# Expert slots that begin behind the last weighing, with the last utterance's routing laid between them

## The chip, the cores and the metric

The kernel runs on one core of a Trainium2 chip. The metric is the device time of one launch in microseconds (us), the median of several launches. Lower is better.

## What is computed

Sixteen utterances of 750 frames with 23 features go through one audio layer. A context-5 projection makes 746 tokens of 128 channels for each utterance, 11,936 in all, with batch normalisation behind it. Then come an attention block with 8 heads of 16 channels and a feed-forward layer with 8 experts, of which each token uses exactly one:

```python
h = _L0_tok_ref(x, W, b, gamma, beta)
h = h + _L0_attn_ref(_layernorm(h), ...)      # softmax(q k^T / 4) v, 8 heads, then Wo
# _L0_ffn_ref(_layernorm(h), ...):
router_logits = xf @ Wr + br
topk_logits, topk_idx = jax.lax.top_k(router_logits, 1)
topk_gates = jax.nn.softmax(topk_logits, axis=1)
for e in range(8):
    hh = jax.nn.relu(xf @ W1[e] + b1[e])      # 128 -> 512
    oe = hh @ W2[e] + b2[e]                   # 512 -> 128
    out = out + jnp.where((idx_k == e)[:, None], gate_k * oe, 0.0)
```

## The kernel before, in words

Every engine has a program of its own, written out by hand; semaphores (`s_...`) tie the programs together. B = 16 utterances, D = 128, NT = 6 token tiles for an utterance, STEPS = 96.

**Bodies.** `run_bodies` writes 19 bodies, i = -2 to 16. Body i runs the 96 attention steps of utterance i on TensorE (score matmuls, L1247, and weighings of the values, L1312), the exponentials on ScalarE (L808), and the score maxima of a coming utterance on VectorE (L1112). Between the steps stand, at numbered places, the projections for utterance i + 2 and the routing of utterance i - 1: output projection (task PROJ), residual, layer norm statistics, router, ranks (task RANK), and six indirect DMAs on GpSimd, which scatter the token rows to `routed_rows_dram`, sorted by expert (L631). Body 16, LAST_BODY, has no attention step of its own: it holds the last weighing's drain and the routing of utterance 15, one instruction after the other.

**Slots.** The sorted rows are worked off in 101 slots of 128 rows with one expert each (`run_slots`, L361). For a slot SyncE loads the rows (L561); TensorE transposes them (`x_t_slot`, L1382), runs `layer1` (L1391, four matmuls) and `layer2` (L1401, four matmuls); ScalarE copies the transpose out (L861) and does the relu (L852, four instructions); VectorE copies the expert's weights, 1,156 numbers a partition, for the slot three further on (L1097), adds the bias (L1209) and applies gate and residual (L1214); GpSimd scatters the result to the output (`store_slot`, L720). Rows and results have a ring of 6 buffers, weights one of 3. VectorE's turn s waits until the store of slot s - 6 has landed, and SyncE's load of slot s until VectorE has finished slot s - 6. In TensorE's turn s stand layer1 of slot s + 1, the transpose of slot s + 2 and layer2 of slot s.

**Two tables** tell which expert and which rows a slot has. The early table covers the slots that are full with what had been ranked when it was made (EARLY = 78 of them, made in body 16 out of utterances 0 to 14). The late table (L1168 to L1192) covers the rest. Slots 0 to 11 are written out; behind slot 5 VectorE makes the late table in one piece, and behind slot 11 it is put in place. Then SyncE writes eight blocks of pad rows (`pad_regions`, L424 and L425) and waits for them before it loads slot 12. Slots 12 up to the last few are a hardware loop (`Fori`) with six slots in its body, on every engine.

## Time and profile before

| | us |
|---|---|
| median of 3 runs (lowest, highest) | 1274.9 (1272.45, 1276.98) |
| profiled execution, span from first to last instruction | 1275.9 |
| TensorE busy in the span | 1178.7 (92%) |
| VectorE busy | 1072.5 (84%) |
| ScalarE busy | 950.6 (75%) |
| GpSimd busy | 680.0 (53%) |

For the profiled execution no device time is listed beside its span; the span lies 1.0 us above the median and inside the three runs. Busy shares are averages over stages with different limits. The bodies end at about 1033 us, and the slots run from 1048 us to the end; the two have to be read apart. In rows of instructions the first two numbers are start and duration, the bracket at the end is the engine's idle time before the row and what released it. PEclk is TensorE's granted clock as a share of 2.4 GHz. "remote" and "issue" mean that the profile shows no releaser on this core.

### The profile page before, as it was taken

The numbers are of one execution on the slowest core, as the hardware profiler recorded it, in microseconds if no ns is written. First come the engines' busy times: TensorE is split into PE (matmuls) and PEld (weight loads), VectorE is DVE, ScalarE is ACT, GpSimd is POOL, SyncE is SP. The second block draws the span as 40 slices with busy tenths as digits, with TensorE's granted clock in tenths as the row PEclk, the third lists the DMA queues.
The fourth block names the chain that finished last, engine by engine and source line by source line (L and its number), as shares of the span: only waits on it lengthen the run. The fifth ranks groups of instructions, "written<-read, shape, count | busy, mean of one in ns | idle before, by whom it ended". The sixth has DMA issues, their size and how long they took to land.

```text
span 1275.9 us, 53879 instructions
## 1 busy us (share of the span) xinstructions
PE 1178.7 (92%) x21379; PEld 745.5 (58%) x21379; DVE 1072.5 (84%) x2756; ACT 950.6 (75%) x2477; POOL 680.0 (53%) x894
## 2 busy tenths in 40 slices
PE   6479999999999999999999999999999846899996
PEld 3334656555555556555555556565644326899996
DVE  7469899999999999999999999999999544577774
ACT  4426988888887878788888878797877824567774
POOL 2062436566473837475665739374723334456664
PEclk9768999999999999999999999999999969899998
DMA  8152132222313131323223131313220513333331
GB/s 190 39 84 79 40 86 72 76 84 61 94 52 94 45 105 42 104 72 79 83 63 93 51 94 45 106 41 104 72 80 28 150 56 105 88 93 105 103 101 50
DMA packets 79409, 102.32 MB, mean 80 GB/s; under 512 B 15916, under 2 KB 72995, under 8 KB 78734
## 3 DMA queue, kind: packets, MB, share of 16 engines
q1 hardware_dynamic: 70624, 79.02, 23.4%
q0 software_dynamic: 8384, 20.22, 5.1%
q8 instruction: 158, 2.59, 0.9%
q14 instruction: 57, 0.47, 0.1%
q10 hardware_dynamic: 186, 0.02, 0.0%
HBM read 60.76 MB, written 38.93 MB: 78 GB/s over the span
## 4 chain that ended last, share of the span: by engine, by line
PE 63%; DVE 20%; issue 5%; POOL 3%; ACT 2%; DMA 1%; SPq 1%; another core or an unknown queue 1%; POOLq 0%; DVEq 0%; ACTq 0%
PE psum L1247 36%; DVE half_max L1112 14%; PE psum L1312 13%; PE psum L1391 6%; PE psum L1401 5%; PE psum L1252 2%; ACT arena L808 2%; DVE stats L916 1%; POOL out_dram L720 1%; DVE rows L990 1%; PE psum L1382 1%; POOL arena L405 1%; DMA arena<-max_rows 1%; PE psum L1267 1%; DVE arena L962 1%
## 5 line engine op out<-in xcount | busy, mean ns | idle before, releaser
L1112 DVE TENSOR_REDUCE half_max<-psum 128x1 f32<-128x373 f32 x1536 | 760.8, 534 | 62.8 <-PE psum L1247 55.0
L808 ACT ACTIVATE arena<-psum 128x373 f32<-128x373 f32 (+1 forms) x1536 | 655.0, 489 | 154.4 <-PE psum L1247 139.0
L1247 PE MATMUL psum<-k_rows,arena 96*32 96x373 bf16 x6144 | 519.1, 329 | 14.9 <-DVE half_max L1112 6.1
L1247 PE MATMUL psum<-arena,k_rows 98*32 98x373 bf16 x6144 | 515.7, 326 | 13.7 <-ACT arena L808 6.2
L1312 PE MATMUL psum<-arena,values 128*32 128x373 f32 (+1 forms) x3072 | 313.2, 478 | 0.2
L1247 PEld LDWEIGHTS psum<-k_rows,arena 96*32 96x32 bf16 x6144 | 173.8, 96 | 195.7 <-DVE half_max L1112 103.4
L1247 PEld LDWEIGHTS psum<-arena,k_rows 98*32 98x32 bf16 x6144 | 176.4, 95 | 178.2 <-ACT arena L808 74.8
L631 POOL DMA_INDIRECT routed_rows_dram<-rows,pos_i x96 | 96.6, 1007 | 170.7 <-PE psum L1247 106.2
L720 POOL DMA_INDIRECT out_dram<-arena,slot_id x101 | 119.2, 1180 | 90.0 <-issue 51.5
L1312 PEld LDWEIGHTS psum<-arena,values 128*32 128x32 f32 (+1 forms) x3072 | 98.4, 110 | 20.7 <-issue 2.8
L861 ACT COPY arena<-psum 128x128 f32<-128x128 f32 x101 | 26.9, 266 | 77.7 <-PE psum L1382 39.7
L639 POOL TENSOR_TENSOR m_diff<-stats 128x6 f32<-128x6 f32 x15 | 3.1, 203 | 147.1 <-DVE stats L916 147.1
L1391 PE MATMUL psum<-arena,seq 128*128 128x128 f32 x544 | 75.3, 283 | 5.1 <-issue 2.4
L852 ACT ACTIVATE arena<-psum,seq 128x128 f32<-128x128 f32 x272 | 77.8, 370 | 0.5 <-issue 0.5
L1401 PE MATMUL psum<-seq,arena 128*128 128x128 f32 x544 | 73.8, 280 | 0.3 <-ACT arena L852 0.3
L1391 PEld LDWEIGHTS psum<-arena,seq 128*128 128x128 f32 x544 | 69.1, 199 | 6.5 <-issue 5.0
L405 POOL TENSOR_SCALAR arena<-h_cur,m_mean,rstd 128x128 f32<-128x128 f32 x90 | 70.9, 800 | 3.3 <-POOL rstd L665 3.3
L405 POOL TENSOR_SCALAR rows<-rows,n_mean,rstd 128x128 f32<-128x128 f32 x90 | 70.8, 796 | 0.0
L1401 PEld LDWEIGHTS psum<-seq,arena 128*128 128x128 f32 x544 | 67.6, 195 | 0.5 <-ACT arena L852 0.5
L1097 DVE COPY seq<-seq 128x1156 f32 x68 | 53.6, 788 | 11.1 <-issue 1.4
L950 DVE STREAM_TRANSPOSE by_tok<-o_un 128x384 f32<-128x384 f32 x64 | 36.2, 566 | 18.7 <-ACT o_un L817 18.7
L1209 DVE TENSOR_TENSOR arena<-psum,seq 128x128 f32<-128x128 f32 x68 | 19.8, 291 | 35.3 <-PE psum L1401 30.9
(218 smaller groups left out, 1447.5 us busy)
## 6 DMA issues: line engine op xcount, KB each, us to landing
arena<-q_parts_dram SPq DMA_DIRECT2D x192, 93.2 KB, 2.4
k_rows<-k_parts_dram SPq DMA_DIRECT2D x192, 93.2 KB, 2.4
arena<-routed_rows_dram SPq DMA_DIRECT2D x101, 130.0 KB
q_parts_dram<-q_part SPq DMA_DIRECT2D x48, 186.5 KB, 2.3
k_parts_dram<-k_part SPq DMA_DIRECT2D x48, 186.5 KB, 2.0
arena<-in_x_t_dram SPq DMA_DIRECT2D x3, 703.1 KB, 14.1
seq<-in_w_dram SPq DMA_DIRECT2D x1, 2048.0 KB
seq<-in_w_dram SPq DMA_DIRECT2D x8, 256.0 KB
```

Of the source, the lines that this page charges most:

```text
L405: last = ops.tensor_scalar(dst(t), src(t), mean_var[:, t, 0:1], r_root[:, t:t + 1], ALU.subtract, ALU.mult)
L631: pool.indirect_dma_start(out=rows_dram, out_offset=bass.IndirectOffsetOnAxis(ap=pos_i[:, t:t + 1], axis=0), in_=rows[:, t, :], in_offset= ...
L720: pool.indirect_dma_start(out=out_rows, out_offset=bass.IndirectOffsetOnAxis(ap=slot_id[:, n:n + 1], axis=0), in_=slot_y[n][:, :], in_offs ...
L808: nc.scalar.activation(probs[0:kn(kt), G % N_P, j, :], st_bank[s % N_ST][0:kn(kt), 0:HALF], ACT.Exp).then_inc(s_exp, 1)
L852: last = nc.scalar.activation(slot_ht[n % 2][:, D * k:D * (k + 1)], psum[:, 2 + n % 2, D * k:D * (k + 1)], ACT.Relu, bias=slot_w[n % N_W][ ...
L950: nc.vector.transpose(by_tok[:, g, first:first + LP // 2], o_un[:, g, first:first + LP // 2])\
L1097: nc.vector.tensor_copy(slot_w[n % N_W].unsqueeze(1), w_sb[:, bass.ds(e, 1), :]).then_inc(s_fw, 1)
L1112: nc.vector.tensor_reduce(half_max[:, m:m + 1], mx_bank[m % N_MX][:, 0:HALF], AX.X, ALU.max)\
L1247: last = nc.tensor.matmul(dst[n:n + m], weights[:, n:n + m], moving, start=start, stop=stop)
L1312: last = nc.tensor.matmul(o_bank[32 * j:32 * (j + 1), first:first + n], values[b % 3][0:kn(kt), kt, GH * (p // 2) + j, :], probs[0:kn(kt), ...
L1391: last = nc.tensor.matmul(psum[:, 2 + n % 2, D * k:D * (k + 1)], slot_w[n % N_W][:, W1 + D * k:W1 + D * (k + 1)], slot_xt[n % 2][:, :], st ...
L1401: last = nc.tensor.matmul(psum[:, 5 + n % 3, 0:D], slot_ht[n % 2][:, D * k:D * (k + 1)], slot_w[n % N_W][:, W2 + D * k:W2 + D * (k + 1)], ...
```

## The change

1. Body 16 is gone. Behind body 15 TensorE runs the last weighing and goes straight to the transposes of slot 0.
2. The routing of utterance 15 is cut in pieces that stand behind numbered slots (the `LATE_...` table): VectorE's transposes in slots 0 to 5, the projection at 8 and 13, residual, layer norm, router and ranks up to slot 40, GpSimd's parts in slots 21 to 38 and its six scatters in slots 43 to 48. The layer norm of these rows is applied by GpSimd instead of VectorE.
3. The early table is made in body 15 (utterances 0 to 13, EARLY = 72), and the weights of slots 0 to 2 are copied there. The late table is cut into six pieces behind slots 42 to 47, the pad rows into four pieces behind loads 50 to 56. Only the load of slot 72 waits for the late scatters, pads and table.
4. All 101 slots are written out on all engines; there is no loop.
5. The slots' buffers move from the ring of exponentials to space that is free during body 15 (`q_rows`, `k_rows`, `values`).

The core of the diff (renamed helpers are left out; `scatter`, `token_ids`, `merge2`, `root2`, `router_logits`, `norm2`, `gate_diff`, `gate`, `out_copy`, `gate_exp` hold the instructions that stood in the bodies before):

```diff
     ROUND = 6
-    EARLY = ((B - 1) * L - E * (D - 1)) // D // ROUND * ROUND
+    EARLY = ((B - 2) * L - E * (D - 1)) // D // ROUND * ROUND
...
+    EARLY_AT, EARLY_T_AT, EARLY_SLOTS_AT, WEIGHTS_AT = 50, 62, 66, (69, 72, 75)
+    LATE_TURN, LATE_INV, LATE_MULT, LATE_BACK = (0, 1), 2, 3, (4, 5)
+    LATE_PROJ, LATE_REST, LATE_LN2 = (8, 13), (10, 15), (16, 17, 18, 19, 20, 21)
+    LATE_IDS, LATE_MERGE, LATE_RSTD, LATE_LOGITS, LATE_NORM = 21, 22, 23, 24, (25, 26, 27, 28, 29, 30)
+    LATE_ROUTE, LATE_RANK, LATE_RANKS = (27, 28, 29, 30, 31, 32), 35, (36, 37, 38, 39, 40)
+    LATE_DIFF, LATE_EXP, LATE_GATE, LATE_SCATTER = 31, 34, 38, (43, 44, 45, 46, 47, 48)
+    LATE_TABLE, LATE_ROWS, LATE_SLOTS = (42, 43, 44, 45, 46, 47), 50, 52
+    PAD_AT = (50, 52, 54, 56)
     N_ST, N_MX, N_P = 3, 3, 3
...
+        def of_q_rows(first, n):
+            return arena[:, RING + first:RING + first + n]
+
+        slot_rows = [of_q_rows(ROW * n, ROW) for n in range(ROUND)]
+        slot_y = [of_q_rows(ROUND * ROW + D * n, D) for n in range(ROUND)]
+        slot_xt = [of_q_rows(ROUND * (ROW + D) + D * n, D) for n in range(2)]
+        slot_ht = [values[1][:, :, :, :].rearrange("p t h c -> p (t h c)")[:, HID * n:HID * (n + 1)] for n in range(2)]
+        slot_w = [seq[:, W_ALL * E:W_ALL * (E + 1)],
+                  k_rows[0][:, :, :].rearrange("p h t -> p (h t)").bitcast(fp32)[:, 0:W_ALL],
+                  values[2][:, :, :, :].rearrange("p t h c -> p (t h c)")[:, 0:W_ALL]]
         slot_id = sb("slot_id", [128, ROUND], i32)
...
-        def run_slots(engine, ahead, turn, behind=None):
-
-
-            for s in range(2 * ROUND):
-                turn(s, s % ROUND, s // ROUND)
-                if behind and s % ROUND == ROUND - 1:
-                    behind(s // ROUND)
-            rounds = (SLOTS - ahead) // ROUND
-            with engine.Fori(2, rounds) as v:
-                for u in range(ROUND):
-                    turn(v * ROUND + u, u, v)
-            for s in range(rounds * ROUND, SLOTS):
+        def run_slots(turn):
+
+
+            for s in range(SLOTS):
                 turn(s, s % ROUND, s // ROUND)
...
             def load_slot(s, n, r):
-                if not isinstance(r, int) or r > 0:
+                if s >= ROUND:
                     sp.wait_ge(s_fy, s - (ROUND - 1))
+                if s == EARLY:
+                    sp.wait_ge(s_scat, B * NT * 16)
+                    sp.wait_ge(s_pad, (E + 1) * 16)
+                    sp.wait_ge(s_tab, TABLES)
                 first = sp.value_load(slot_r_i[0:1, bass.ds(s, 1)], min_val=0, max_val=DEAD)
                 sp.dma_start(slot_rows[n][:, :], rows_dram[bass.ds(first, D), :]).then_inc(s_in[n], 16)
-
-            sp.wait_ge(s_pv, B * GROUPS)
+                if s in PAD_AT:
+                    e = PAD_AT.index(s) * 2
+                    pad_regions(sp, (e, e + 1))
+
+            sp.wait_ge(s_st, (B - 1) * STEPS)
             sp.wait_ge(s_early_tab, 1)
-            sp.wait_ge(s_scat, (B - 1) * NT * 16)
-            for s in range(2 * ROUND):
-                load_slot(s, s % ROUND, s // ROUND)
-            pad_regions(sp, range(E))
-            sp.wait_ge(s_scat, B * NT * 16)
-            sp.wait_ge(s_pad, (E + 1) * 16)
-            with sp.Fori(2, EARLY // ROUND) as v:
-                for u in range(ROUND):
-                    load_slot(v * ROUND + u, u, v)
-            sp.wait_ge(s_tab, TABLES)
-            with sp.Fori(EARLY // ROUND, SLOTS // ROUND) as v:
-                for u in range(ROUND):
-                    load_slot(v * ROUND + u, u, v)
-            for s in range(SLOTS // ROUND * ROUND, SLOTS):
-                load_slot(s, s % ROUND, s // ROUND)
+            sp.wait_ge(s_scat, (B - 2) * NT * 16)
+            run_slots(load_slot)
...
+            scatter_ready(B - 2)
+            for t in range(NT):
+                scatter(t)
+
+            def late(s):
+
+                r = B - 1
+                if s == LATE_IDS:
+                    token_ids(r)
+                if s == LATE_MERGE:
+                    merge2(r)
+                if s == LATE_RSTD:
+                    root2(r)
+                if s == LATE_LOGITS:
+                    router_logits(r)
+                if s in LATE_NORM:
+                    norm2(LATE_NORM.index(s))
+                if s == LATE_DIFF:
+                    gate_diff(r)
+                if s == LATE_GATE:
+                    gate(r)
+                if s == LATE_SCATTER[0]:
+                    scatter_ready(r)
+                if s in LATE_SCATTER:
+                    scatter(LATE_SCATTER.index(s))
...
+            out_copy(B - 1, 3)
...
+                if s == LATE_EXP:
+                    gate_exp(B - 1)
...
+                dve.wait_ge(s_st, (B - 1) * STEPS)
+                dve.wait_ge(s_pv, (B - 1) * GROUPS)
...
-                if is_body(i, LAST_BODY):
-                    early_table()
                 for s in range(STEPS):
-                    if is_body(i, LAST_BODY) and s == BACK_AT[1] + 1:
-                        early_slots()
-                    if is_body(i, LAST_BODY) and s == LN2_AT[-1] + 1:
-                        weights(expert_of(0), 0)
+                    if is_body(i, B - 1):
+                        if s == EARLY_AT:
+                            early_table()
+                        if s == EARLY_SLOTS_AT:
+                            early_slots()
+                        if s in WEIGHTS_AT:
+                            n = WEIGHTS_AT.index(s)
+                            weights(expert_of(n), n)
                     b, m = maximum_of(i, s)
                     if 0 <= b < B:
                         dve.wait_ge(s_mx, b * STEPS + (m + 1))
@@ -1142,12 +1209,6 @@
                             dve.wait_ge(s_free, fill(i, "PROJ", 1))
...
+            def late(s):
+
+                i, r = LAST_BODY, B - 1
+                if s in LATE_TURN:
+                    turn(r, 1, LATE_TURN.index(s))
+                if s == LATE_INV:
+                    inverse(r, 1)
+                if s == LATE_MULT:
+                    normalise(r, 1)
+                if s in LATE_BACK:
+                    turn_back(r, LATE_BACK.index(s))
+                if s in LATE_REST:
+                    residual(i, r, LATE_REST.index(s))
+                if s == LATE_LN2[0]:
+                    dve.wait_ge(s_free, fill(i, "PROJ", 1))
+                    wait(dve, s_ln2_p, ln2_p_done(r))
+                if s in LATE_LN2:
+                    layer_stats(LATE_LN2.index(s), rows, stats2, s_ln2)
+                if s in LATE_ROUTE:
+                    router(i, r, LATE_ROUTE.index(s) + 1)
+                if s in LATE_RANKS:
+                    ranks(i, r, LATE_RANKS.index(s))
+                if s in LATE_TABLE:
+                    late_table(LATE_TABLE.index(s))
+                if s == LATE_SLOTS:
+                    late_slots()
...
-                    if is_body(i, LAST_BODY) and s == WEIGH_AT[-1] - PASS + 1:
+                    if is_body(i, B - 1) and s == EARLY_T_AT:
+                        pe.wait_ge(s_red, B * STEPS)
                         pe.wait_ge(s_early, EARLIES)
                         nc.tensor.transpose(tab_bank[0:1, 0:D], early_e[:, :], ident[:, :])
                         nc.tensor.transpose(tab_bank[0:1, D:2 * D], early_r[:, :], ident[:, :]).then_inc(s_early_t, 1)
...
-            pe.wait_ge(s_free, fill(LAST_BODY, "RANK", 0))
-
-            def late_rows(r):
-                if r == 1:
+            weigh(B - 1, GROUPS - 1, 0)
+
+            def late(s):
+
+                if s == LATE_PROJ[0]:
+                    pe.wait_ge(s_early_tab, 1)
+                if s in LATE_PROJ:
+                    task(LAST_BODY, 0, "PROJ", LATE_PROJ.index(s))
+                if s == LATE_RANK:
+                    task(LAST_BODY, 0, "RANK", 0)
+                if s == LATE_ROWS:
+                    pe.wait_ge(s_free, fill(LAST_BODY, "RANK", 0))
                     pe.wait_ge(s_tab, TABLES - 1)
                     nc.tensor.transpose(tab_bank[0:1, 0:D], slot_e[:, :], ident[:, :])
                     nc.tensor.transpose(tab_bank[0:1, D:2 * D], slot_r[:, :], ident[:, :]).then_inc(s_tab_t, 1)
 
             def x_t_slot(s, n, r):
                 pe.wait_ge(s_in[n], r * 16 + 16)
...
+                if s == 1:
+                    pe.wait_ge(s_o, B * 4)
+                if s == 2:
+                    pe.wait_ge(s_free, fills_before(LAST_BODY))
...
             def pe_turn(s, n, r):
-                if not isinstance(s, int) or s + 1 < SLOTS:
+                if s + 1 < SLOTS:
                     layer1(s + 1, n + 1)
-                if not isinstance(s, int) or s + 2 < SLOTS:
+                if s + 2 < SLOTS:
                     x_t_slot(*later(s, n, r, 2))
                 layer2(s, n)
+                late(s)
 
```

**TensorE, from the end of the last weighing (values 32x373) to the first slots.** Before (`wo_wr` is the output projection, `onehot` and `zero_b` the ranks, `ident,arena` 128x128 a slot's transpose, `arena,seq` layer1):

```order
L1312 MATMUL psum<-arena,values 32x373 x8
L1361 MATMUL psum<-ident,early_e 1x128
L1362 MATMUL psum<-ident,early_r 1x128
L1247 MATMUL psum<-wo_wr,merged_t 32x136 x24
L1247 MATMUL psum<-onehot,before 32x56 x4
L1247 MATMUL psum<-onehot,ones_b 32x48 x4
L1247 MATMUL psum<-onehot,ones_b 32x40 x4
L1247 MATMUL psum<-onehot,ones_b 32x32 x4
L1247 MATMUL psum<-onehot,ones_b 32x24 x4
L1247 MATMUL psum<-onehot,ones_b 32x16 x4
L1247 MATMUL psum<-onehot,ones_b 32x8 x4
L1247 MATMUL psum<-zero_b,ones_b 32x56 x4
```

Now the first slots follow the weighing (L1481 transpose, L1490 layer1, L1504 layer2):

```order
L1405 MATMUL psum<-arena,values 32x373 x8
L1481 MATMUL psum<-ident,arena 128x128
L1490 MATMUL psum<-arena,seq 128x128 x4
L1481 MATMUL psum<-ident,arena 128x128
L1490 MATMUL psum<-arena,k_rows 128x128 x4
L1481 MATMUL psum<-ident,arena 128x128
L1504 MATMUL psum<-seq,values 128x128 x4
```

The projection and the ranks have moved behind layer2 of slots 8, 13 and 35, and the early table's transposes into body 15.

**GpSimd, slots 22 to 31 (the stores of 24 to 29, each with one `rows` piece behind it, are alike).** Before, all stores stood one behind the other (L720). Now:

```order
L771 DMA out_dram<-arena,slot_id 11936x128
L681 TENSOR_TENSOR n_diff<-stats 128x6
L682 TENSOR_TENSOR n_both<-stats 128x6
L683 TENSOR_TENSOR n_ss<-stats 128x6
L685 TENSOR_SCALAR n_half<-n_diff 128x6
L686 TENSOR_SCALAR n_mean<-n_both 128x6
L687 TENSOR_SCALAR n_var<-n_ss 128x6
L689 TENSOR_TENSOR n_diff<-n_half 128x6
L691 TENSOR_TENSOR var_eps<-n_diff,n_var 128x6
L771 DMA out_dram<-arena,slot_id 11936x128
L646 TENSOR_TENSOR rstd<-var_eps,minus_half 128x6
```

```order
L771 DMA out_dram<-arena,slot_id 11936x128
L661 TENSOR_SCALAR rows<-rows,n_mean,rstd 128x128
L771 DMA out_dram<-arena,slot_id 11936x128
L669 TENSOR_TENSOR g_diff<-top 128x6
L771 DMA out_dram<-arena,slot_id 11936x128 x7
```

Moments and root of utterance 15 stand behind slots 22 and 23, its layer norm behind 25 to 30, and the gate's difference `g_diff` behind slot 31.

**ScalarE, around slot 34 (L922 copies a transpose out, L913 is the relu, L861 the exponential of the gate).** Before, the exponential stood ahead of all slots; now:

```order
L922 COPY arena<-psum 128x128
L913 ACTIVATE values<-psum,k_rows 128x128 x4
L861 ACTIVATE g_exp<-g_diff 128x6
L922 COPY arena<-psum 128x128
L913 ACTIVATE values<-psum,values 128x128 x4
```

The exponential has moved behind the relu of slot 34 and ahead of the copy for slot 36; it needs GpSimd's `g_diff` of slot 31.

## Rows read from the trace of the kernel before

**Rows 1.** The page: span of the profiled execution.

```profile
span 1275.9 us, 53879 instructions
```

**Rows 2.** Stretches: start:end, length, busy PE, PEld, DVE, ACT, POOL, PEclk, DMA share, GB/s.

```profile
1025.00:1030.00 5.00, 1.97 (x20) 0.51 (x20) 0.00 (x0) 1.55 (x4) 2.78 (x4) 0.61 0.30 104
1035.00:1040.00 5.00, 2.92 (x48) 2.49 (x48) 3.13 (x10) 0.00 (x0) 0.00 (x0) 0.66 0.06 19
...
1110.00:1120.00 10.00, 7.57 (x43) 7.57 (x44) 3.43 (x10) 4.18 (x15) 2.92 (x3) 0.66 0.18 51
...
1150.00:1160.00 10.00, 10.00 (x92) 10.00 (x91) 7.76 (x21) 7.17 (x26) 6.45 (x6) 1.00 0.37 106
```

**Rows 3.** Timeline, all engines, from the last weighing to slot 0.

```profile
1031.55 2.09 PE L1312 MATMUL psum<-arena,values 128*32 128x373 f32 x16
...
1033.72 0.47 ACT L817 COPY o_un<-psum 128x373 f32<-128x373 f32 x1 [1.39 <-PE psum L1312]
...
1036.95 2.92 PE L1247 MATMUL psum<-wo_wr,merged_t 128*32 128x136 f32 x48 [3.00 <-DVE merged_t L971]
...
1048.46 0.47 PE L1382 MATMUL psum<-ident,arena 128*128 128x128 f32 x1 [1.30 <-DVE next_row L1035]
...
1049.38 2.05 PE L1391 MATMUL psum<-arena,seq 128*128 128x128 f32 x8 [0.45 <-ACT arena L861]
```

**Rows 4.** Timeline, TensorE: layer2 of slot 0, transpose of 12, layer1 of 23.

```profile
1053.77 1.06 PE L1401 MATMUL psum<-seq,arena 128*128 128x128 f32 x8
...
1084.32 0.47 PE L1382 MATMUL psum<-ident,arena 128*128 128x128 f32 x1 [6.08 <-DMA arena<-routed_rows_dram]
...
1112.43 2.07 PE L1391 MATMUL psum<-arena,values 128*128 128x128 f32 x8 [3.46 <-ACT arena L861]
```

**Rows 5.** Timeline, TensorE, layer2 of slots 40, 98 and 100.

```profile
1150.42 1.06 PE L1401 MATMUL psum<-seq,arena 128*128 128x128 f32 x8
...
1260.43 1.06 PE L1401 MATMUL psum<-values,arena 128*128 128x128 f32 x8
...
1263.62 1.16 PE L1401 MATMUL psum<-seq,arena 128*128 128x128 f32 x8 [0.34 <-ACT arena L852]
```

**Rows 6.** Timeline, the three pauses of ScalarE, with GpSimd's start just ahead of the third.

```profile
1028.03 0.48 ACT L808 ACTIVATE arena<-psum 128x373 f32<-128x373 f32 x1 [2.48 <-remote]
...
1060.33 0.27 ACT L861 COPY arena<-psum 128x128 f32<-128x128 f32 x1 [3.15 <-remote]
...
1106.16 1.10 POOL L720 DMA_INDIRECT out_dram<-arena,slot_id  x1 [2.69 <-issue]
...
1112.04 0.27 ACT L861 COPY arena<-psum 128x128 f32<-128x128 f32 x1 [4.35 <-remote]
```

**Rows 7.** GpSimd by group: count, busy us and mean ns, idle before.

```profile
L720 POOL DMA_INDIRECT out_dram<-arena,slot_id x101 | 119.2, 1180 | 90.0 <-issue 51.5 <-DVE arena L1214 38.5
L631 POOL DMA_INDIRECT routed_rows_dram<-rows,pos_i x96 | 96.6, 1007 | 170.7 <-PE psum L1247 106.2 <-DVE pos_i L1046 56.7 <-issue 7.9
...
L405 POOL TENSOR_SCALAR rows<-rows,n_mean,rstd 128x128 f32<-128x128 f32 x90 | 70.8, 796 | 0.0
...
L710 POOL TENSOR_TENSOR g_inv<-g_exp,minus_one 128x6 f32<-128x6 f32 x16 | 22.1, 1379 | 11.9 <-ACT g_exp L838 11.9
...
L639 POOL TENSOR_TENSOR n_diff<-stats 128x6 f32<-128x6 f32 x15 | 3.1, 209 | 50.7 <-DVE stats L916 50.7
```

**Rows 8.** Timeline, VectorE and GpSimd, one settled slot.

```profile
1152.64 0.35 DVE L1214 SCALAR_TENSOR_TENSOR arena<-arena 128x128 f32<-128x128 f32 x1
...
1153.42 0.29 DVE L1209 TENSOR_TENSOR arena<-psum,values 128x128 f32<-128x128 f32 x1 [0.31 <-PE psum L1401]
1153.86 0.81 DVE L1097 COPY values<-seq 128x1156 f32 x1
...
1152.01 1.56 POOL L720 DMA_INDIRECT out_dram<-arena,slot_id  x1 [0.96 <-issue]
1153.88 0.98 POOL L720 DMA_INDIRECT out_dram<-arena,slot_id  x1 [0.30 <-issue]
```

**Rows 9.** Timeline, SyncE: the eight pad blocks.

```profile
1070.82 8.67 SPq L425 DMA_DIRECT2D routed_rows_dram<-pad_row  x8
```

189 lines of the change are left out of this document (96 added, 93 removed).

## The prediction, written before the change was run

> **What bounds the kernel now.** I read the end first, since the change touches nothing ahead of body 15. In the page's chain of waits TensorE holds most of the span, so I asked for TensorE's stretches with its clock, then for the timelines.
>
> In the settled slots TensorE has no gap at all: 10.00 of 10.00 us busy, clock 1.00, against 7.76 on VectorE, 7.17 on ScalarE and 6.45 on GpSimd [rows 2]. From layer2 of slot 40 (1150.42) to that of slot 98 (1260.43) go 58 slots: 1.897 us a slot. The last two take 3.19 us together [rows 5]. If all slots ran so, layer2 of slot 0 to that of slot 100 would be 98 x 1.897 + 3.19 = 189.1 us. It is 1263.62 - 1053.77 = 209.85 us [rows 4, 5]: 20.75 us are lost inside the slots. And ahead of them the last weighing ends at 1033.64, while the first transpose starts at 1048.46 [rows 3]: 14.8 us in which one utterance's routing runs alone, with TensorE busy for little more than its projection.
>
> Where the 20.75 us went: the transpose of slot 12 waited 6.08 us for its rows [rows 4], which SyncE could load only behind the pad blocks (1070.82 to 1079.49 [rows 9]). Two pauses of ScalarE, 3.15 and 4.35 us long, have no releaser on this core [rows 6]; behind the second, TensorE had been idle for 3.46 us [rows 4]. A gap costs more than itself: in 1110 to 1120 the clock was 0.66, half way between the levels of 1.2 and 2.4 GHz [rows 2], and layer1 took 2.07 us where a settled group of eight records takes 1.06 [rows 4, 5]. The rest is waiting around the late table.
>
> **The change, part by part.** The sum is made against the profiled span, 1275.9 us [rows 1], 1.0 us above the median of the runs.
>
> *Removed: the routing ahead of the slots.* Slot 0's transpose can follow the weighing at once, but its copy on ScalarE stands behind the output copy of 1033.72 to 1034.19 [rows 3]. So layer1 of slot 0 starts near 1034.6 instead of 1049.38: -14.8 us. Its rows and the weights of slots 0 to 2 are fetched in body 15, where VectorE was idle (0.00 busy in 1025 to 1030 [rows 2]). Bounds: -15.8 (warmer clock at the start) to -12 (a pause as at 1028 at the same place). Layer2 of slot 0: about 1039.
>
> *Removed: the stalls in the slots.* Pads and late table no longer stand in front of slot 12, the loop is gone. If nothing waits, the slots take 189.1 us: -20.75.
>
> *Moved onto TensorE between slots.* Two projections took 2.92 us at a clock of 0.66 [rows 2, 3], 1.9 at full clock; the ranks and two transposes are small beside it, 0.3 by my estimate. TensorE has no idle time, so all of it is on the path: +2.2 (bounds 1.9 and 3.4).
>
> *Moved onto VectorE.* Before its bias add it has 0.31 us of idle a slot [rows 8]. The weights of slot s + 3 end at 1154.67 when layer1 of s + 3 follows about 0.5 us later, so a piece may last some 0.8 us before TensorE sees it. The pieces are one or a few operations each. Only slots 0 to 5, with a transpose each, can add up. +0.5 (0 to 3).
>
> *Moved onto SyncE.* Eight pad blocks took 8.67 us [rows 9], 1.1 each, two behind each of four loads. Each pair delays the next load by about 2.2 us less the queue's idle time of about 0.9; a load has some 1.5 us to spare. The delays add up over the four pairs: +0.7 (0 to 4).
>
> *Moved onto GpSimd, and what waits for it.* A store takes 1.18 us on average, 0.98 or 1.56 in single rows, with 0.30 between two that follow at once [rows 7, 8]. I take 1.27 a store, the lower of the two, since the queue then runs without VectorE's step between: 0.63 us spare a slot. From slot 22 to 30 stand eight small operations (0.2 each, 1.9 with their waits), a root (1.38), two on the logits (0.6) and six norms of 0.80 [rows 7]. Walked slot by slot with slot 21's result at 0: store 21 ends at 1.9; moments 5.8; store 23 and root 8.5; logits 10.5; six times 2.1 for store and norm, 23.1; store 31 and `g_diff` 24.6. ScalarE reaches the exponential of slot 34 at 13 x 1.9 less the 2.9 us by which its relu leads VectorE's result, at 21.8. It is an in-order engine: behind the exponential stand the copy for slot 36 and thus TensorE's layer1. ScalarE waits 2.8 us, of which about 0.5 is slack: +2.3 on the path. Bounds: 0, and 7.5 if stores take 1.56 and the gap then costs clock as in rows 4. The six scatters at 43 to 48 (1.0 + 0.3 each [rows 7]) lag GpSimd by 6 x 0.65 = 3.9 us; a store has about 5.6 us before slot s + 6 needs its buffer, so they cost nothing (up to 3 without that cover).
>
> *Pauses that no row explains.* ScalarE has three [rows 6]; in the timeline GpSimd issues several DMAs in a row near each. Ahead of the third, GpSimd itself is late by 2.69 us, at the start of the loop's second pass [rows 6]. The new order still has such runs (six scatters ahead of the slots, twelve DMAs around slot 45). I keep one, +3.0; bounds 0 and two of 6.5 (3.46 plus about 3 at low clock).
>
> What the Trainium skill says on this: by Runtime: NRT & Kernel Launch, section Instruction fetch mechanics, a taken branch whose target is outside the fetched window stalls for the fetch, while straight code is fetched ahead. The 2.69 us at the loop's second pass would fit; the two pauses in written-out code do not. By that rule alone the term is 0 and the time 1245.
>
> Sum: 1275.9 - 14.8 - 20.75 + 2.2 + 0.5 + 0.7 + 2.3 + 3.0 = 1249.05 on the span, less 1.0: **1248 us**. With every term at its good end 1240 (no waits in the slots, 1.9 on TensorE), with the GpSimd terms and pauses at their bad ends 1265.
>
> **Rivals.**
> *A: GpSimd becomes the bound of slots 21 to 48.* If each DMA there costs 1.56 + 0.30 = 1.86 us [rows 8], 28 slots leave 1 us spare in all, and the late work is 6 x 1.86 + 4.8 + 2.8 + 3 = 21.8 us. The ring hides 5.6 of it: 15 us on the path where the sum has 2.3, so 1261. For: 1.56 is not rare (mean 1.18 against 0.98). Against: 1.56 came when a store met VectorE's copy, and the store that began a run without gaps at 1106 took 1.10 [rows 6]. The Trainium skill speaks for this one: SBUF — State Buffer, section SBUF: two separate sides, has VectorE's fp32 copy lock GpSimd out of a shared port so that it cannot write its descriptors. The trace shows 0.6 us of that on some stores, not all; by the rule on every store, 1261.
>
> *B: the pauses come back in straight code.* More code streams in: 85 slots more on each engine. If three pauses of 6.5 us fall in the slots, 1248 - 3 + 19.5 = 1264. For: two of three fell in written-out code. Against: bodies 0 to 14 are written out too, with more TensorE instructions a microsecond, and ScalarE's timeline has no such pause in them.
>
> *C: slower. TensorE stays at the low clock level.* If a small wait comes in every slot, e.g. for weights or for the copy behind a busy ScalarE, TensorE never runs without a gap, and a slot takes 2.85 us instead of 1.90 (2.07 against 1.06 for a group [rows 4, 5], mixed), 0.95 more. The removed time is some 28 us net, so it decides from 30 slots; over 60 slots it gives 1305. For: every clock fall in rows 2 began with a gap. Against: the written-out slots 0 to 11 of before, the same chain, ran at clock 1.0 where nothing was late.
>
> *D: the stalls only move.* The start is earlier by 14.8 but slot 72 waits for late table, pads or scatters as slot 12 did, with its slow clock, about 9 us, beside the terms above: 1257. Against: they are done by slot 56, sixteen slots or 30 us ahead.
>
> **How the numbers follow.** Forecast 0.70, A 0.10, B 0.10, D 0.05, C 0.05. The range 1239 to 1264 takes in forecast, D, most of A and half of B. A measurement tells about 0.3% (4 us) from no change; all cases but C lie 10 us or more below 1274.9: faster 0.94, same 0.01, slower 0.05.
>
> **What would show it.** Layer2 of slot 0 near 1039 (not above 1042). No TensorE wait for rows at slot 12; 1.90 us a slot outside slots 30 to 50. ScalarE waiting 2 to 3 us for GpSimd's `g_diff` at slot 34. GpSimd's rows between slots 22 and 31 without gaps above 0.3. No wait of SyncE at slot 72. Layer2 of slot 100 near 1237. Wrong would be: GpSimd named as releaser of VectorE's slot_id copies over many slots (A), "remote" or "issue" gaps of over 2 us on ScalarE (B), a granted clock under 1 for more than 20 us in the slots (C).

## The result, and the profile of the changed kernel

The changed kernel takes 1261.05 us (median of four runs, 1258.58 to 1262.69) where the kernel before took 1275.52 beside it: ratio 0.990, 95% interval 0.988 to 0.992. It is faster by 14.5 us; the forecast was 27.

The page and the stretches that answer to [rows 1, 2] (same columns):

```profile
span 1256.4 us, 52556 instructions
```

```profile
1025.00:1035.00 10.00, 8.11 (x71) 7.78 (x70) 6.42 (x19) 5.24 (x21) 6.27 (x6) 1.00 0.33 96
...
1080.00:1110.00 30.00, 21.53 (x180) 20.89 (x177) 14.20 (x43) 11.86 (x46) 23.94 (x22) 0.79 0.25 73
...
1140.00:1160.00 20.00, 15.31 (x100) 14.75 (x100) 8.74 (x26) 7.38 (x30) 10.42 (x10) 0.74 0.38 115
1160.00:1170.00 10.00, 10.00 (x92) 10.00 (x91) 7.36 (x22) 7.03 (x27) 6.01 (x5) 1.00 0.38 110
```

From 1160 us on TensorE has no gap, as before in its settled slots. It lacks 8.5 of 30 us in 1080 to 1110 and 4.7 of 20 in 1140 to 1160, and there its mean clock is low too (0.79 and 0.74).

The hand-over, answering to [rows 3] (timeline, TensorE and ScalarE), then TensorE's layer 2 of slots 99 and 100 [rows 5]:

```profile
1019.03 1.78 PE L1405 MATMUL psum<-arena,values 128*32 128x373 f32 x16
1020.74 0.33 PE L1481 MATMUL psum<-ident,arena 128*128 128x128 f32 x1
1020.88 0.47 ACT L855 COPY o_un<-psum 128x373 f32<-128x373 f32 x1 [0.95 <-PE psum L1405]
1021.24 0.27 ACT L922 COPY arena<-psum 128x128 f32<-128x128 f32 x1
1021.66 1.13 PE L1490 MATMUL psum<-arena,seq 128*128 128x128 f32 x8 [0.59 <-ACT arena L922]
...
1024.42 1.06 PE L1504 MATMUL psum<-seq,values 128*128 128x128 f32 x8
```

```profile
1242.29 1.06 PE L1504 MATMUL psum<-seq,values 128*128 128x128 f32 x8
1243.68 1.16 PE L1504 MATMUL psum<-k_rows,values 128*128 128x128 f32 x8 [0.34 <-ACT values L913]
```

The slots begin as forecast, right behind the last weighing. But layer 2 of slot 0 to that of slot 100 now takes 1243.68 - 1024.42 = 219.3 us, 9.4 more than the 209.85 of before and 30.2 more than the ideal 189.1. Against 1.897 us a slot, the losses are (each by the start of layer 2 of the slots named): slots 2-3 2.4 us, slots 9 and 14 (a projection each) 1.0 each, slots 30-31 6.5, slots 35-36 7.8, slots 45-54 11.5; from slot 55 on nothing.

At slots 30 and 35 GpSimd's results are late (timeline, GpSimd: the end of its moments, the root, one of the six norms and `g_diff`; then single rows of those who waited):

```profile
1077.83 0.79 POOL L691 TENSOR_TENSOR var_eps<-n_diff,n_var 128x6 f32<-128x6 f32 x1
1081.78 1.52 POOL L771 DMA_INDIRECT out_dram<-arena,slot_id  x1 [3.16 <-issue]
1083.33 1.38 POOL L646 TENSOR_TENSOR rstd<-var_eps,minus_half 128x6 f32<-128x6 f32 x1
...
1093.45 1.42 POOL L661 TENSOR_SCALAR rows<-rows,n_mean,rstd 128x128 f32<-128x128 f32 x1
1095.05 1.07 POOL L771 DMA_INDIRECT out_dram<-arena,slot_id  x1 [0.17 <-issue]
...
1104.86 0.20 POOL L669 TENSOR_TENSOR g_diff<-top 128x6 f32<-128x6 f32 x1
```

```profile
1086.66 0.20 DVE L1065 TENSOR_REDUCE top<-logits 128x6 f32<-128x48 f32 x1 [4.04 <-POOL logits L655]
...
1088.78 2.08 PE L1490 MATMUL psum<-arena,k_rows 128*128 128x128 f32 x8 [3.86 <-DVE k_rows L1162]
...
1105.09 0.21 ACT L861 ACTIVATE g_exp<-g_diff 128x6 f32<-128x6 f32 x1 [5.60 <-POOL g_diff L669]
...
1105.55 2.05 PE L1490 MATMUL psum<-arena,seq 128*128 128x128 f32 x8 [4.62 <-issue]
```

At slots 45-54 nobody waits for GpSimd's results. GpSimd starts its DMAs 1.28 to 1.83 us after one another from 1129 to 1149, and ScalarE and VectorE get TensorE's results late (timeline; TensorE's transpose for the copy at 1143.92 is recorded at 1140.05):

```profile
1140.95 0.29 DVE L1301 TENSOR_TENSOR arena<-psum,k_rows 128x128 f32<-128x128 f32 x1 [2.87 <-remote]
...
1143.92 0.27 ACT L922 COPY arena<-psum 128x128 f32<-128x128 f32 x1 [3.90 <-issue]
...
1146.10 0.29 DVE L1301 TENSOR_TENSOR arena<-psum,values 128x128 f32<-128x128 f32 x1 [3.63 <-remote]
...
1149.06 0.27 ACT L922 COPY arena<-psum 128x128 f32<-128x128 f32 x1 [3.83 <-remote]
```

These are rows of the kind of [rows 6]. The question for the experiments was what makes them.

### The profile page after: what moved, and what is told of

It reads as the page before. It is cut to its first block, busy times and chain, and to the rows that moved or that the text cites. A ratio compares the mean times of both kernels' runs of the same rounds, so it can differ in the third digit from the quotient of the medians.

```text
span 1256.4 us, 52556 instructions
## 1 busy us (share of the span) xinstructions
PE 1172.1 (93%) x21379; PEld 741.3 (59%) x21379; DVE 1063.9 (85%) x2742; ACT 941.5 (75%) x2477; POOL 690.8 (55%) x908
## 4 chain that ended last, share of the span: by engine, by line
PE 62%; DVE 17%; issue 7%; POOL 6%; ACT 2%; DMA 1%; POOLq 0%; SPq 0%; DVEq 0%; ACTq 0%
PE psum L1340 38%; PE psum L1405 13%; DVE half_max L1179 12%; POOL out_dram L771 4%; PE psum L1490 4%; PE psum L1504 3%; PE psum L1345 2%; ACT arena L873 2%; DVE stats L979 1%; DVE rows L1053 1%; POOL arena L408 1%; PE psum L1360 1%; DMA arena<-max_rows 1%; PE psum L1481 0%; DVE neg_max L998 0%
## 5 line engine op out<-in xcount | busy, mean ns | idle before, releaser
L922 ACT COPY arena<-psum 128x128 f32<-128x128 f32 x101 | 26.8, 265 | 84.0 <-PE psum L1481 52.1
L661 POOL TENSOR_SCALAR rows<-rows,n_mean,rstd 128x128 f32<-128x128 f32 x96 | 78.5, 826 | 0.4
L1490 PE MATMUL psum<-arena,k_rows 128*128 128x128 f32 x272 | 38.3, 286 | 8.7 <-issue 4.4
L1490 PE MATMUL psum<-arena,seq 128*128 128x128 f32 x272 | 38.1, 285 | 6.5 <-issue 5.9
L1490 PEld LDWEIGHTS psum<-arena,k_rows 128*128 128x128 f32 x272 | 34.5, 199 | 10.0 <-issue 5.7
L913 ACT ACTIVATE values<-psum,k_rows 128x128 f32<-128x128 f32 x136 | 39.0, 376 | 0.5 <-issue 0.5
L1490 PEld LDWEIGHTS psum<-arena,seq 128*128 128x128 f32 x272 | 34.7, 200 | 7.3 <-issue 7.3
L913 ACT ACTIVATE values<-psum,seq 128x128 f32<-128x128 f32 x136 | 39.0, 377 | 0.0
L1490 PE MATMUL psum<-arena,values 128*128 128x128 f32 x264 | 36.6, 284 | 2.0 <-issue 1.9
```

The source lines that it names most:

```text
L661: op = nc.gpsimd.tensor_scalar(rows[:, t, D:2 * D], rows[:, t, 0:D], n_mean[:, t:t + 1], rstd2[:, t:t + 1], ALU.subtract, ALU.mult)
L913: last = nc.scalar.activation(slot_ht[n % 2][:, D * k:D * (k + 1)], psum[:, 2 + n % 2, D * k:D * (k + 1)], ACT.Relu, bias=slot_w[n % N_W][ ...
L1490: last = nc.tensor.matmul(psum[:, 2 + n % 2, D * k:D * (k + 1)], slot_w[n % N_W][:, W1 + D * k:W1 + D * (k + 1)], slot_xt[n % 2][:, :], st ...
```

## Experiments

All times are given as the ratio to the kernel before on the same chip. The number that tells more is the time in the slots, from layer 2 of slot 0 to that of slot 100, since the start of slot 0 itself stood between 1024.4 and 1030.6 us in eighteen profiled runs whose work up to there is nearly the same. The profiled run of the changed kernel, at 1024.4, is the earliest of them.

| kernel | ratio [95%] | in the slots, us |
|---|---|---|
| before | 1 | 209.9 |
| changed | 0.990 [0.988, 0.992] | 219.3 |
| e1_exp_later | 0.990 [0.988, 0.992] | 218.5 |
| e2_route_later | 0.991 [0.989, 0.993] | 217.6 |
| e3_scatter_spread | 0.992 [0.990, 0.994] | 219.3 |
| e4_scatter14_spread | 0.996 [0.995, 0.998] | 226.7 |
| e5_scatter_burst | 0.991 [0.989, 0.993] | 219.4 |
| e6_dose | 1.003 [1.001, 1.005] | 235.5 |
| e7_norm_dve | 0.987 [0.985, 0.989] | 212.3 |
| e8_both | 0.987 [0.986, 0.989] | 216.5 |
| e9_deep | 0.992 [0.991, 0.994] | 220.9 |
| e10_deep_norm | 0.988 [0.985, 0.991] | 215.8 |
| e11_dose_deep | 1.003 [0.999, 1.007] | 241.3 |
| e12_shallow | 0.994 [0.992, 0.996] | 226.5 |
| e13_kinds | 0.998 [0.996, 1.000] | 228.2 |
| e14_before_dose | 1.020 [1.017, 1.024] | 237.3 |
| e15_paced | 1.014 [1.010, 1.018] | 233.7 |
| e16_late_light | 0.986 [0.984, 0.988] | 210.7 |
| e17_paced_fourth | 0.988 [0.986, 0.990] | 213.9 |
| e18_every_fourth | 0.988 [0.986, 0.989] | 215.5 |

**1. Moving single pieces.**

```
e1: LATE_EXP 34 -> 39, LATE_GATE 38 -> 42
e2: LATE_ROUTE 27..32 -> 31..36, LATE_RANK 35 -> 37, LATE_RANKS 36..40 -> 38..42
e3: LATE_SCATTER 43..48 -> 43, 46, 49, 52, 55, 58
e4: the six scatters of utterance 14, before slot 0 -> one behind each of stores 0 to 5
```

> The changed kernel with ScalarE's exponential of the last utterance moved from slot 34 to slot 39 and GpSimd's gate from 38 to 42; nothing else. Theory G (GpSimd's pieces for the last utterance end late, and an engine that is placed too soon behind them waits): the wait of 5.60 us at slot 35 goes, slots 35-36 lose at most 1 us instead of 7.7, and the time is 1254 us (1252 to 1257). Theory U (the straight code itself makes the engines pause, at about the same places): the pause stays or moves by a slot, 1261 us. Theory B (GpSimd is the bound of slots 30 to 54 as a whole, so a wait that goes comes back further on): slots 45-54 lose 6 us more than 11.5 and the time is 1259 to 1261 us.

> The changed kernel with the last utterance's router steps on VectorE moved from slots 27-32 to 31-36 and the ranks with them (37, 38-42); GpSimd's and ScalarE's pieces stand where they stood. Theory G: VectorE's wait of 4.04 us for the logits at slot 27 goes, slots 30-31 lose 0 to 1.5 us instead of 6.5; the difference of the gates can come no sooner than before, so slots 35-36 lose as much as before: 1255 us (1253 to 1258). Theory U: unchanged, 1261 us, with PE and DVE waits of issue or remote kind at slot 30. Theory B: 1259 to 1261 us, since the loss comes back at slots 45-54.

> The changed kernel with the last utterance's six scatters behind the stores of slots 43, 46, 49, 52, 55 and 58 instead of 43 to 48. Theory R (a run of GpSimd's indirect DMAs without a gap makes completions reach the other engines 2 to 4 us late, pauses of 'remote' and 'issue' kind): GpSimd has gaps again behind each store, and of the 11.5 us that slots 45-54 lose at least 8 go: 1251 us (1249 to 1254). Theory B (work of GpSimd as such): the scatters cost GpSimd the same 7 us wherever they stand, the backlog from slot 35 is worked off between them, and 3 to 6 us go: 1257 us. Theory T (the late table on VectorE and the pads on SyncE, in slots 42 to 56, are what is waited for): unchanged, 1261 us.

> The changed kernel with the six scatters of the last utterance but one, which stood back to back ahead of the first slot's store, put one behind each of the stores of slots 0 to 5. Theory R: the pause of slots 2-3 (2.3 us, just behind seven DMAs in a row) goes: 1259 us (1257.5 to 1260.5), and layer 2 of slots 0 to 8 comes every 1.90 us. Theory U (instruction supply of straight code, or the change from utterances to slots itself): the pause of 2.3 us stays where it is, 1261 us.

None of the forecasts of the theories G (GpSimd's results come late) and R (runs of its DMAs delay others) held: e1, e2 and e3 stayed near 1261 us, which is what the other theories had said, and e4 was slower than any had it. In e1 the wait of 5.60 us was gone, yet slots 36-40 lost 4.8 us, with a "remote" pause of 3.02 us, where slots 35-36 had lost 7.8. In e2 slots 30-31 lost nothing, slots 32-38 lost 11.4 (ScalarE now waited 9.49 us for `g_diff`) and slots 44-53 13.7: the loss moved. In e3 slots 46-66 lost 13.2 us, in a rhythm: four DMAs, a scatter among them, starting 1.27 to 1.44 us apart, then a pause. One round of it (timeline, GpSimd's four DMAs with one row of TensorE and one of VectorE; the other rows between them are left out; columns as in [rows 8]):

```profile
1161.95 1.14 POOL L771 DMA_INDIRECT out_dram<-arena,slot_id  x1 [3.04 <-DVE arena L1306]
1163.39 1.00 POOL L628 DMA_INDIRECT routed_rows_dram<-rows,pos_i  x1 [0.30 <-issue]
1163.87 1.06 PE L1504 MATMUL psum<-k_rows,values 128*128 128x128 f32 x8
1164.69 0.97 POOL L771 DMA_INDIRECT out_dram<-arena,slot_id  x1 [0.30 <-issue]
1165.96 0.97 POOL L771 DMA_INDIRECT out_dram<-arena,slot_id  x1 [0.30 <-issue]
1167.60 0.29 DVE L1301 TENSOR_TENSOR arena<-psum,k_rows 128x128 f32<-128x128 f32 x1 [3.02 <-remote]
```

Layer 2 is recorded from 1163.87 to 1164.93; VectorE's add, which waits for that alone, came 2.7 us later. The next round had its pause at 1175.63; after the last scatter there was none. In e4 six scatters among stores cost 8.5 us at slots 4-7, where the six in a row had been followed by 2.4.

**2. Scatters in one run; norms on VectorE; both.**

```
e5: if s == 43: for t in range(NT): scatter(t)
e7: norm2(t) on VectorE at slots 28..33 instead of on GpSimd at 25..30
e8: e5 and the norms on VectorE at 32..37; router 30..35, ranks 37..42, exp 36, gate 39
```

> The changed kernel with the last utterance's six scatters all behind the store of slot 43, in a row, instead of one behind each of slots 43 to 48. In the runs so far a scatter between two stores cost about 2 us wherever it stood (11.5 us for six at slots 43-48, 13.4 at 43-58, 8.5 at slots 0-5), and the six of utterance 14 in a row ahead of the first store 1.2 to 4.1 us in all. Theory R (each scatter between stores closes GpSimd's gap for three to four DMAs and sets off a pause of about 3 us; in a row they are over before the stores pile up): the six cost 3 to 6 us, 1255 us (1252 to 1258). Theory B (GpSimd's work as such, in whatever order): unchanged, 1261 us, with the wait at VectorE's next use of a stored row.

> The changed kernel with the last utterance's six norms on VectorE (0.34 us each, slots 28 to 33) instead of GpSimd (0.79 to 1.42 us each, slots 25 to 30). Theory G+R (the norms, stretched by VectorE's copies, make GpSimd 5.6 us late with the difference of the gates, and the stores that follow without a gap set off a pause): of the 7.7 us at slots 35-36 at least 6 go, up to 1 us comes from VectorE: 1255 us (1252 to 1258). Theory B: the backlog of GpSimd comes from the stores and scatters, and the loss turns up at slots 45-54: 1259 to 1261 us.

> Both of these together (norms on VectorE, at slots 32 to 37, the six scatters in a row behind slot 43), with the router at slots 30-35, the ranks at 37-42, the exponential at 36 and the gate at 39. Theory G+R: slot 30 loses nothing (6.5 before), slots 35-36 nothing (7.7), the scatters 3 to 6 instead of 11.5: 1243 us (1240 to 1248). Theory B: 1258 to 1261 us.

e5: 12.4 us at slots 45-53, no gain. e7 is the first that held: slots 35-37 lost 0.7 us instead of 7.8, the rest hardly changed, and the time in the slots fell by 7.0. So the norms on GpSimd caused that loss. The rule of the Trainium skill (SBUF — State Buffer, SBUF: two separate sides) that VectorE's copy and GpSimd's operation exclude each other on a shared port agrees: the norms took 1.29 us on average in the slots against 0.80 [rows 7]. e8 missed by 14 us: without the wait at slot 30, VectorE ran into GpSimd's backlog itself and waited 3.22 us for a store to land, and the pauses followed (8.9 us at slots 32-35, 13.6 at 45-57).

**3. Extra work in settled slots, where nothing else is lost.**

```
e6:  store of slot 62, 68: + 1 indirect DMA of 128 rows; slot 74: + 2
     slot 82: + 1 power on GpSimd, slot 86: + 2; SyncE, loads 93, 94: + 1 direct DMA each
```

> The changed kernel with extra work put into slots that run at 1.897 us each: behind the stores of slots 62 and 68 one more indirect DMA of GpSimd of the scatter's size (into memory that nothing reads), behind that of slot 74 two in a row, behind 82 one power operation on GpSimd (some 1.4 us) and behind 86 two, and on SyncE behind the loads of slots 93 and 94 one direct DMA of 133 KB each. Theory R: a single extra DMA costs 1.5 to 2.5 us within four slots, the two in a row 2 to 4 us, a power operation, which makes the following stores come without a gap too but is no DMA, 0 to 2.5 us (0 if the number of DMAs matters, as much as a DMA if the lack of gaps does), SyncE's DMAs nothing. Theory B: every one of them costs nothing, since GpSimd has 0.7 us left per slot and six buffers ahead. Time 1261 to 1272 us.

The extra DMAs cost 3.9, 2.2 and (two) 4.3 us, each a few slots later; 1.4 us were lost at slot 88 and 4.5 at slots 93-94. The time, 1276.6 us, lay above the range forecast. An extra DMA is over after 1.27 us on an engine with 0.63 us to spare a slot, yet one costs two or three times its length. The first one (timeline, GpSimd, TensorE, ScalarE):

```profile
1177.27 1.53 POOL L790 DMA_INDIRECT out_dram<-arena,slot_id  x1 [0.96 <-DVE arena L1325]
1179.10 0.97 POOL L779 DMA_INDIRECT dose_dram<-rows,pos_i  x1 [0.31 <-issue]
1180.38 0.97 POOL L790 DMA_INDIRECT out_dram<-arena,slot_id  x1 [0.30 <-issue]
1181.66 1.12 POOL L790 DMA_INDIRECT out_dram<-arena,slot_id  x1 [0.30 <-issue]
1183.08 0.97 POOL L790 DMA_INDIRECT out_dram<-arena,slot_id  x1 [0.30 <-issue]
```

```profile
1181.24 0.27 PE L1500 MATMUL psum<-ident,arena 128*128 128x128 f32 x1
...
1184.41 1.13 PE L1509 MATMUL psum<-arena,values 128*128 128x128 f32 x8 [2.00 <-issue]
```

```profile
1184.04 0.27 ACT L941 COPY arena<-psum 128x128 f32<-128x128 f32 x1 [3.08 <-remote]
```

I took this for a load that lands late, since SyncE's DMAs seemed to cost as much, and tested that. I had also put the 1.4 us at slot 88 down to the pair of powers and taken the single power for free; so the texts of e9 below say. The rows show otherwise: layer 2 of slot 88 was late before the pair began (timeline, single rows):

```profile
1226.54 1.70 POOL L784 TENSOR_TENSOR dosed<-g_exp,minus_one 128x6 f32<-128x6 f32 x1
...
1233.40 0.27 ACT L941 COPY arena<-psum 128x128 f32<-128x128 f32 x1 [2.20 <-remote]
...
1234.85 1.08 PE L1523 MATMUL psum<-k_rows,values 128*128 128x128 f32 x8
...
1235.62 3.47 POOL L784 TENSOR_TENSOR dosed<-g_exp,minus_one 128x6 f32<-128x6 f32 x2
```

So the 1.4 us belong to the single power at 1226.54, which three stores 1.27 to 1.38 us apart followed.

**4. Are the loads late?**

```
e9:  DEEP = 9 buffers for the token rows (sp.wait_ge(s_fy, s - (DEEP - 1))), pads at loads 53..59
e10: e9 and e7        e11: e6 and e9        e12: DEEP = 5
```

> The changed kernel with nine buffers for the slots' token rows instead of six, so that each load of 133 KB is issued three slots (5.7 us) sooner; the pads go with the loads 53 to 59 instead of 50 to 56, so at the same slots. Theory L (the pauses that the profile calls 'remote' are TensorE waiting for a load that lands late, because scatters, pads or bunched stores of the same size share the DMA engines: one extra DMA in a settled slot, by GpSimd or by SyncE, cost 2.3 to 3.9 us four to five slots later, a power operation of 1.4 us nothing): the 2.3 us at slots 2-3 stay or go, of the 11.5 us at slots 45-54 at least 9 go, slots 30 and 35 keep most of their 6.5 and 7.7 us (they wait for GpSimd's results): 1250 us (1246 to 1253). Theory R (completions of TensorE reach the others late whenever GpSimd issues DMAs without a gap): unchanged, 1261 us.

> Nine buffers and the six norms on VectorE (slots 28 to 33). Theory L with G (GpSimd late by its norms): the two gains add, 9 to 12 us from slots 45-54 and 6 from slots 35-36: 1244 us (1240 to 1248). Theory R: 1256 us, as with the norms alone.

> The kernel with extra DMAs in settled slots (one behind the stores of 62 and 68, two behind 74, powers behind 82 and 86, two direct DMAs of SyncE with the loads of 93 and 94), with nine buffers. Theory L: none of the extra DMAs costs more than 0.5 us, where they cost 3.9, 2.3, 4.3 and 4.5 with six buffers, and the time is that of nine buffers alone, about 1250 us. Theory R: they cost what they did, and the time is 15 us above that of nine buffers.

> The changed kernel with five buffers instead of six, each load issued one slot later. Theory L: the load has 1.9 us less, every disturbance turns into a pause and the settled slots too may miss 1.897 us: at least 1270 us. Theory R: the settled slots keep 1.897 us if the load is in time, and the pauses are the same ones: 1261 us.

No. With three more slots of time for every load, slots 45-57 lost 12.6 us, and the extra DMAs of e11 cost 4.7, 4.0 and 4.2 us. My theory fell. e12, with a slot's time less, lost 4.4 us in slots 55-98, where the changed kernel loses none, and 1.4 at slot 5: its loads were late only now and then. Its 1270.1 us are not a sign for theory L, since the kernel before took 1277.5 on that chip; the ratios, 0.994 and e9's 0.992, lie close together. e10 lost 5.0 us less in the slots than e9, as e7 lost 7.0 less than the changed kernel.

**5. What kind of work, what kind of code, what spacing.**

```
e13: slot 60: + 3 powers; slot 68: + 1 indirect DMA of 16 rows; SyncE, loads 82: + 1, 90: + 2 direct
     DMAs of 133 KB; slot 92: + 1 direct DMA by GpSimd
e14: the kernel before, + 1 indirect DMA in every round of six slots (n == 0), 14 of 15 in the loop
e15: e6's DMAs at slots 62, 70, 78, 86, and from slot 58 a small operation with a wait behind each store
```

> The changed kernel with four kinds of extra work in settled slots, one at a time: three power operations on GpSimd behind the store of slot 60 (some 4.2 us, after which the stores come without a gap, but no DMA more), an indirect DMA of 16 rows instead of 128 behind slot 68, a direct DMA of 133 KB by SyncE with the load of slot 82 (issued at slot 76) and two with that of slot 90 (issued at slot 84), and a direct DMA issued by GpSimd behind slot 92. Theory R (what makes TensorE stop for 2.4 to 3 us is GpSimd issuing four or more indirect DMAs 0.30 us apart, whatever they move): the powers cost 2 to 4 us in a pause some four slots later, the small DMA as much as a full one (2.3 to 3.9 us), SyncE's DMAs nothing. Theory Q (what counts is bytes on the DMA engines): the powers and the small DMA cost nothing, SyncE's cost 2 to 4 us each. Time 1261 us plus 4 to 10.

> The kernel before with one more indirect DMA of the scatter's size in each round of six slots (behind the store of slots 6, 12, ... 90; fourteen of the fifteen in the rolled loop). Theory R: every one costs 2 to 4 us though GpSimd has four slots to catch up, 1305 to 1325 us. Theory U (pauses come from code that is written out): none in the loop, at most 1279 us.

> The changed kernel with one more indirect DMA behind the stores of slots 62, 70, 78 and 86, and from slot 58 on a small operation of some 0.2 us on GpSimd behind every store, so that a run of DMAs comes 0.5 to 0.6 us apart instead of 0.30. Theory R, if the gap decides: the four cost under 1 us each. If it is the number of DMAs within some microseconds, or any DMA beyond one a slot: 2.3 to 3.9 us each, as without the small operations, 9 to 15 us in all.

e13 took 1269.8 us, within theory R's 1265 to 1271. The three powers, which add no DMA, cost 5.9 us; the DMA of 16 rows 2.0; none of the direct DMAs anything, three of SyncE's and one of GpSimd's. So bytes are not the cause, and the 4.5 us at the end of e6 were not SyncE's: GpSimd stood in a run of four stores there, behind the pair of powers. One power, two and three thus cost 1.4, 4.5 and 5.9 us. (GpSimd's direct DMA took 0.64 us, and no stores close together followed it; what it would do in a run is not shown.) The powers held GpSimd until 1181.6; then came six stores 1.27 us apart, and the result of a layer 2 recorded from 1184.08 to 1185.14 was used at 1190.25 (timeline, GpSimd and TensorE, then VectorE):

```profile
1181.64 1.06 POOL L790 DMA_INDIRECT out_dram<-arena,slot_id  x1 [0.91 <-DVE arena L1325]
1183.01 0.97 POOL L790 DMA_INDIRECT out_dram<-arena,slot_id  x1 [0.30 <-issue]
...
1188.10 0.97 POOL L790 DMA_INDIRECT out_dram<-arena,slot_id  x1 [0.30 <-issue]
1192.58 1.32 POOL L790 DMA_INDIRECT out_dram<-arena,slot_id  x1 [3.51 <-DVE arena L1325]
```

```profile
1184.08 1.06 PE L1523 MATMUL psum<-k_rows,values 128*128 128x128 f32 x8
...
1189.13 1.50 PE L1509 MATMUL psum<-arena,seq 128*128 128x128 f32 x8 [4.00 <-issue]
```

```profile
1190.25 0.29 DVE L1320 TENSOR_TENSOR arena<-psum,k_rows 128x128 f32<-128x128 f32 x1 [3.27 <-remote]
```

e14: fifteen extra DMAs cost 27.5 us in the slots, 1.8 each, fourteen of them in rolled code: a little under theory R's 2 to 4, and far from nothing. Code that is written out is not needed for it.

e15: with 0.9 us between the DMAs there was not one "remote" wait behind slot 58, and the first extra DMA cost 0.2 us. But a store with its small operation took mostly 2.2 to 2.7 us, more than a slot, so GpSimd became the bound, slots 59-98 lost 14.7 us, and VectorE waited for stores to land:

```profile
1206.58 0.15 DVE L1313 COPY slot_id<-arena 128x1 int32<-128x1 int32 x1 [3.12 <-DMA out_dram<-arena,slot_id]
```

**6. Less for GpSimd, and spacing that it can afford.**

```
e16: norms on VectorE 34..39, token numbers 14, merge 22, root 25, logits 28, router 32..37,
     ranks 39..43, difference 34, exp 37, gate 41, scatters 46..51, table 44..49
e18: e16 with LATE_SCATTER = (44, 48, 52, 56, 60, 64)
e17: e18 and, for 44 <= s < 70, behind each store and scatter
     nc.gpsimd.tensor_scalar(spare[...], var_eps2, 1.0, 0.0, ALU.mult, ALU.add), no wait
```

> The changed kernel with GpSimd's work for the last utterance thinned: norms on VectorE (slots 34-39), token numbers at slot 14, merge 22, root 25, logits 28, router 32-37, ranks 39-43, difference 34, exponential 37, gate 41, scatters 46-51, late table 44-49. Theory G+R: slots 30-36 lose at most 3 us of their 14, the scatters cost 11 to 13 us as before since each closes the gap: 1251 us (1248 to 1255). Theory B: 1256 us or more, since GpSimd, once as many as six stores behind, holds VectorE back.

> The kernel e16_late_light with the six scatters behind the stores of slots 44, 48, 52, 56, 60 and 64 and, from slot 44 to 69, a small operation of some 0.2 us on GpSimd behind each store and each scatter, for which nothing waits, so that DMAs in a run start some 1.5 us apart instead of 1.27. Theory R, with the spacing of the starts as what decides (runs 1.27 us apart stop TensorE, runs 1.6 us and more apart did so little in the changed kernel at 1122 to 1134 us): the 11.6 us that e16 loses in slots 47-58 shrink to 0 to 4, 1246 us (1243 to 1250). If 1.5 us is still too dense, or GpSimd falls six stores behind: 1254 us or more.

> The same with the scatters at the same slots and without the small operations. Theory R: each scatter is followed by stores 1.27 us apart and costs about 2 us wherever it stands, 11 to 13 us in all, 1254 us. If what counts is only how many DMAs beyond one a slot come close together (rival): one in four slots is rare enough, 1245 us.

e16 has the lowest ratio of the case, 0.986, and the shortest slots, 210.7 us; the 0.987 of e7 and e8 can't be told from it. Its 1254.0 us lie in the range forecast. Slots 30-40 lose 6.1 us instead of 14.3, slots 47-58, with the scatters, 11.1. In e18 slots 47-69, with the scatters at every fourth, lost 13.7 us, no less than the 11.1 of e16, where they stand close together. In e17, at the same slots but with a small operation between the DMAs, slot 47 lost 3.9 us, behind a run whose starts were still 1.3 to 1.5 us apart (1126.29 to 1131.84), slots 48-54 lost 2.6, where four DMAs started 1.45 to 1.56 us apart, and slots 55-69 nothing, three scatters among them, with all starts 1.72 to 1.90 us apart. The stretch 1140 to 1180, with five scatters in it:

```profile
1140.00:1180.00 40.00, 38.95 (x345) 38.52 (x345) 29.09 (x88) 26.36 (x102) 34.37 (x45) 1.00 0.43 124
```

Its total, 1261.2 us, is no better than e18's 1260.8 on the same chip and missed the 1246 forecast, because the last scatter was issued at 1179.53, and the load of slot 72, which waits for all scatters, came late: 7.1 us at slots 70-72.

```profile
1185.23 0.47 PE L1489 MATMUL psum<-ident,arena 128*128 128x128 f32 x1 [4.37 <-DMA arena<-routed_rows_dram]
```

The same with scatters that begin and end two or three slots earlier wasn't tried; by e17's rows I estimate that it would save most of those 7.1 us.

## Why the prediction was right and wrong

*Removed: the routing ahead of the slots (-14.8).* Right. From the last weighing's start to layer 2 of slot 0 went 53.77 - 31.55 = 22.2 us, now 24.42 - 19.03 = 5.4: -16.8, at clock 1.00. The profiled run was another 12.5 us ahead at the start of that weighing: 3.5 us at the first attention body, 3.7 won in the bodies up to 1020 us, and 5.4 in the stretch of [rows 2] with the first pause of [rows 6]. The first two are differences between runs, so luck. The third is not: that pause stood behind the six scatters of utterance 14 in a row (1020.74 to 1027.28), and in the changed kernel these start at 1020.87, behind the last weighing, so the pause comes in slots 2-3, where it costs 2.4.

*Removed: the stalls in the slots (-20.75).* The waits named did go: no wait for rows at slot 12, no wait around the late table, settled slots at 1.897 us in straight code as in the loop.

*Moved onto TensorE (+2.2).* Right: slots 9 and 14 lost 1.0 each. *VectorE (+0.5), SyncE (+0.7):* no wait names them; what they cost can't be told apart from the rest.

*Moved onto GpSimd, and what waits for it (+2.3).* This step failed. Measured: 6.5 us at slots 30-31, 7.8 at 35-36, 11.5 at 45-54, 25.8 in all. Three errors:
- `g_diff` ended 33.8 us behind slot 21's result instead of 24.6, and ScalarE waited 5.60 us for it, not 2.8. Of the 9.2 us too little 3.16 are GpSimd's stop ahead of store 23, and 2.9 (six times 0.49) come from the norm, priced at 0.80 us from bodies in which VectorE copies no weights; it took 1.29. The rest is in the moments and stores. e7 shows that the norms on GpSimd as such cost 7.1 of the 7.8 us; what 0.80 us a norm would have cost is not shown.
- the wait of VectorE for the logits (4.04 us) was not seen at all: the router was placed three slots behind the logits, and GpSimd stood 3.16 us ahead of store 23 (a stop like that of 2.69 in [rows 6]). In e2 and e16, with the router later, slot 30 loses nothing, though in e2 the loss came back behind it.
- "they cost nothing" of the six scatters: the queue did have buffers to spare, and no store was waited for. But a backlog that is worked off makes a run of DMAs 1.27 us apart, and in such runs TensorE's results arrive late. That is 1.8 to 4.7 us for each extra DMA (e3, e6, e11, e14, e18), 11.5 for the six.

*Pauses that no row explains (+3.0).* The term was there and its cause, "GpSimd issues several DMAs in a row near each", stood beside it, but it was taken as chance and not tied to the backlog worked out just above. At slots 2-3, behind the six scatters of utterance 14, 2.4 us.

Sum in the slots: forecast 189.1 + 8.7 = 197.8, measured 219.3, so 21.5 us more than forecast. Slot 0's layer 2 came 14.6 us sooner than the forecast 1039, and the end behind slot 100 took 0.4 more: together the 7.3 us between the forecast span (1249.05) and 1256.4. The total missed by 13.0 us; the other 5.7 come from the way from span to median: the sum took 1.0 us off, but this run's device time, 1258.58, is 2.2 above its span, and the median is 2.5 above this run. So the slots missed by more than the total shows, and the early start of slot 0, in part luck, hides it.

*Readings that do not hold.* The 2.69 us of [rows 6] do not stand at the start of the loop's second pass, but ahead of the store of slot 17, the last of the first pass, and the changed kernel, which has no loop, has such a stop as well. And "1.56 came when a store met VectorE's copy" is half of it. The copy beside [rows 8] is

```profile
1151.96 0.76 DVE L1097 COPY seq<-seq 128x1156 f32 x1
```

The store of 1152.01, 0.05 us behind its start, took 1.56 us; that of 1153.88, 0.02 us behind the start of the next copy, 0.98. From 1120 to 1260 us of the kernel before, 41 DMAs that start within 0.04 us of the start of such a copy took 0.97 or 0.98 us, and 32 that start 0.05 to 0.08 behind it 1.53 to 1.56. So meeting the copy alone did not make a store slow; a few hundredths of a microsecond in its start did.

The 0.66 in 1110 to 1120 is not "half way" between the levels: the clock stood at 1.2 GHz for 6.8 of the 10 us and at 2.4 for the rest. And the bad end of the sum is 1266 rather than 1265 (5.2 and 3 more on GpSimd, 10 for the pauses).

*Rivals.* A gave the right time, 1261, by another mechanism: in the changed kernel no wait of VectorE names a store, and a DMA took 1.19 us on average, not 1.56. It is what e15 made happen. B's pauses came back, but not from straight code (e14). C was wrong, though its sign came: the clock was at its lower level, 1.2 GHz, for 23.9 us of the slots, in three stretches (from 1087.0, 1104.1 and 1145.0), each behind a wait; between and behind them it was 2.4 GHz and a slot 1.897 us. D was wrong: SyncE did not wait at slot 72, until e17 put a scatter at 64.

## What to carry to other kernels

Work moved to an engine that "has 0.6 us to spare a slot" is not free until what it does while it catches up is looked at: here the catching up cost more than the work. Price an operation from rows where its new neighbours run beside it. And when pauses without a releaser stand in a profile, list what every other engine does in the microseconds before each: all three of the kernel before stood behind the same pattern, and one extra DMA in quiet slots showed the price in one run.

## What the runs showed of the hardware

- Three or more indirect DMAs of GpSimd that start 1.2 to 1.5 us apart, mostly 1.27 to 1.30, are followed by TensorE's results reaching ScalarE and VectorE late: 1.4 to 5 us behind the recorded end of the matmul at the extra DMAs and powers (e3, e6, e11, e13, e14, e18), up to 7.1 in longer runs (e13, slots 51-53). In e14 three DMAs are enough. In the changed kernel's own run from 1129 to 1149 us the starts were mixed, 1.28 to 1.83 us apart. At 1.72 to 1.90 us apart, with an operation between them, there was no loss (e17, slots 55-69), nor a "remote" wait at mostly 2.2 to 2.7 us (e15).
- In the slots of all twenty profiled kernels there are 110 such runs (starts up to 1.5 us apart), and at or behind 92 of them a result is late by 1.3 us or more. Of the other 18, eleven stand where ScalarE waited for `g_diff` and the chain was at rest anyway.
- It needs neither extra DMAs (the powers of e6 and e13) nor written-out code (e14). More load buffers do not take it away (e9), and SyncE's direct DMAs do not bring it about (e13). The profile calls the wait "remote" on ScalarE and VectorE and "issue" on TensorE, or names the matmul, which is recorded at the early time. In e6 and e13 the results came in the last DMA of the run, at 1184.04 and 1188.77. What links the two engines in the hardware is open.
- GpSimd stops for 3.16 us ("issue") in the changed kernel and in sixteen of the seventeen made from it, after 113 of its scatters and stores; in e4 for 3.30, and the kernel before has its 2.69 of [rows 6], after 113 as well. In e14 GpSimd is idle for 5.53 us after 113, extra DMAs counted, but there the profile names VectorE's result. The cause is open.
